# A graph network and attention kernel on one core: later steps for the aggregates and projections of two slots, and a gather moved ahead of a scatter

## What is computed

```python
h = jnp.maximum(_layernorm(x, axis=-1), 0.0)
x = x + _L0_gnn_ref(adj, h, L0_gnn_W, L0_gnn_b)      # gather of up to 25 rows, maximum, linear, relu
h = jnp.maximum(_layernorm(x, axis=-1), 0.0)
x = x + _L1_gnn_ref(h, adj, L1_gnn_Wqkv, ...)        # attention over adj | adj.T | eye, then the feed-forward part

# inside _L0_gnn_ref
scores = jnp.where(mask, pri, neg_inf)
vals, idx = jax.lax.top_k(scores, S)                 # S = 25: the lowest neighbour indices
feats = jax.vmap(lambda x, i: x[i])(X, idx)
agg = feats.max(axis=2)
out = jax.nn.relu(jnp.einsum('bnf,fo->bno', h, W) + b)

# inside _L1_gnn_ref
scores = jnp.where(allowed[:, None], scores, -jnp.inf)
attn = jax.nn.softmax(scores, axis=-1)
```

## Time and profile before

| | |
|---|---|
| timed executions, us | 1256.07, 1257.35, 1259.07; median 1257.35 |
| span of the profiled execution, us | 1257.3 (no other time is given for it; its span is within 0.05 of the median) |
| busy, share of the span | TensorE 84%, VectorE 64%, ScalarE 64%, GpSimd 59% |
| chain that ended last | TensorE 63%, ScalarE 11%, VectorE 9%, GpSimd 7%, issue 6%, DMA 3% |
| mean granted TensorE clock | 0.933 |

### The profile page before, as it was taken

How to read it: one execution, slowest core, us unless ns; L and a number is a source line. 1 busy time by engine, 2 the same in 40 slices (tenths; PEclk the granted TensorE clock), 3 DMA queues, 4 the chain that set the end, 5 groups by cost and what they waited for, 6 DMA issues and landing times.

```text
span 1257.3 us, 29309 instructions
## 1 busy us (share of the span) xinstructions
PE 1051.1 (84%) x10998; PEld 407.3 (32%) x10998; DVE 809.0 (64%) x3062; ACT 805.9 (64%) x1031; POOL 737.5 (59%) x741
## 2 busy tenths in 40 slices
PE   0136687688993989999999999999999999999874
PEld 0122331243331433343434333434343334333222
DVE  7866887758778476977797869776364534122323
ACT  1221257677852767788878887888768756875541
POOL 4776677567777777777777777777777520000000
PEclk9556789899997899999999999999999999999996
DMA  6523336416322534353435343532242210000000
GB/s 188 167 69 105 93 103 158 147 53 137 119 83 80 140 85 135 104 121 85 131 112 115 87 129 107 120 86 62 78 69 71 55 52 18 18 3 10 10 9 8
DMA packets 95157, 110.77 MB, mean 88 GB/s; under 512 B 17081, under 2 KB 75969, under 8 KB 94977
## 3 DMA queue, kind: packets, MB, share of 16 engines
q1 hardware_dynamic: 68352, 62.67, 16.4%
q0 software_dynamic: 22816, 44.61, 15.6%
q10 hardware_dynamic: 3808, 1.19, 0.4%
HBM read 91.10 MB, written 12.85 MB: 83 GB/s over the span
## 4 chain that ended last, share of the span: by engine, by line
PE 63%; ACT 11%; DVE 9%; POOL 7%; issue 6%; DMA 3%; DVEq 0%; POOLq 0%; ACTq 0%; SPq 0%
PE sc L1673 20%; PE cb L1693 13%; ACT probs L1469 10%; PE sc L1677 7%; PE m L1749 5%; PE m L1757 4%; POOL nb_low L716 3%; POOL nb_low L694 3%; PE m L1579 2%; PE m L1602 2%; PE sc L1715 1%; DMA nb_low<-h_rows,lsorted 1%; PE m L1731 1%; PE m L1607 1%; PE m L1779 1%
## 5 line engine op out<-in xcount | busy, mean ns | idle before, releaser
L1469 ACT ACTIVATE probs<-sc 128x1024 f32<-128x1024 f32 x512 | 496.5, 1022 | 247.6 <-PE sc L1677 245.6
L694 POOL DMA_INDIRECT nb_low<-h_rows,lsorted x474 | 470.1, 992 | 172.3 <-issue 126.1
L1693 PE MATMUL cb<-probs,va 128*17 128x512 f32 x2048 | 272.3, 604 | 4.8 <-issue 4.1
L1673 PE MATMUL sc<-q_near,k_g 32*128 32x512 f32 x1024 | 147.8, 644 | 21.7 <-ACT probs L1469 18.5
L1673 PE MATMUL sc<-q_far,k_g 32*128 32x512 f32 x1024 | 149.6, 654 | 16.3 <-ACT probs L1469 15.9
L1016 DVE TENSOR_REDUCE agg<-nb_low 128x128 f32<-128x1024 f32 (+10 forms) x58 | 96.4, 1662 | 54.3 <-DMA nb_low<-h_rows,lsorted 31.5
L1677 PE MATMUL sc<-barred,negident 32*32 32x512 bf16 x4096 | 112.9, 388 | 0.3 <-issue 0.2
L830 DVE MAX8 cand<-keys 128x8 f16<-128x128 f16 x512 | 105.4, 279 | 2.2
L716 POOL DMA_INDIRECT nb_low<-h_rows,first_lists x80 | 80.1, 1001 | 42.5 <-issue 23.2
L1677 PEld LDWEIGHTS sc<-barred,negident 32*32 32x32 bf16 x4096 | 35.4, 88 | 198.6 <-issue 198.6
L1461 ACT ACTIVATE barred<-m 128x512 bf16<-128x512 f32 x128 | 73.4, 610 | 40.6 <-PE m L1607 40.6
(11 more groups left out here) (182 smaller groups left out, 1457.6 us busy)
## 6 DMA issues: line engine op xcount, KB each, us to landing
adj_t<-in_adj_dram SPq DMA_DIRECT2D x64, 512.0 KB
nb_low<-h_rows,lsorted POOLq DMA_INDIRECT x474
xh<-in_x_dram SPq DMA_DIRECT2D x8, 512.0 KB
h_rows<-xh SPq DMA_DIRECT2D x8, 512.0 KB
hl<-h_rows SPq DMA_DIRECT2D x8, 512.0 KB
x<-in_x_dram SPq DMA_DIRECT2D x16, 256.0 KB
out_dram<-h2T SPq DMA_DIRECT2D x16, 256.0 KB
ag<-pooled_rows SPq DMA_DIRECT2D x7, 512.0 KB
```

The lines of the kernel that those rows point to most:

```text
L694: pool.indirect_dma_start(out=dst, out_offset=None, in_=h_rows[0:(f + 1) * (N + 1), :], in_offset=bass.IndirectOffsetOnAxis(ap=lsorted[:, ...
L1469: nc.scalar.activation(probs[:, i % 2, 2 * pair:2 * pair + 2, :], sc[:, 2 * pair:2 * pair + 2, :], ACT.Exp, scale=SCALE).then_inc(s_probs, 1)
L1673: nc.tensor.matmul(sc[:, a, :], k[part, :], q[part, :], start=True, stop=False)
L1693: last = nc.tensor.matmul(cb[a * SPAN:a * SPAN + VW, :], va[:, u % 2, a, kt, :], probs[:, i % 2, a, :], start=(kt == 0), stop=(kt == T - 1))
```

## The change

Six things are moved; no instruction is added or taken away except register instructions.

1. Slot 0, graph 1: the transposes of `ag` go from step 22 to 24, the linear layer from 23, 24 to 25, 26, the transposes behind it from 27 to 28, the projections from two a step in 28 and 29 to two a step in 29 and 30, the value rows from 30 to 31.
2. Slot 0, graph 2: the two TensorE steps of its ranks (the transpose of `full` and the rank counts) go from 19 and 21 to 21 and 23.
3. Slot 0, graph 3: ScalarE applies the first norm in steps 27 and 28, not 22 and 23 (`H_AT_0`), and on VectorE `first_norm(3)` stands behind `linear(1)`, not ahead of it; `list_tile(3, 2)` goes behind `flag(1)`, and the adjacency loads are set around `store_h_rows(3)` and `turn_values(1, 0)`.
4. Slot 1, graph 2: the transposes of `ag` go from step 20 to 23, the linear layer from 21, 22 to 24, 25, the transposes behind it from 25 to 27, the projections from one a step in 26 to 29 to two a step in 28 and 29.
5. Slot 1 on VectorE: `add_input(0, 1)` ahead of `pool_tile(2, 6)`, `list_tile(4, 2)` behind `pool_tile(2, 7)`, and graph 3's `pool_tile(3, 0)` and `(3, 1)` behind `flag(2)`.
6. GpSimd, graph 2 only: tile 7 is gathered ahead of `scatter_lists(3)`; the scatter is cut in two around `send(2, 7)`, and `load_lists(3)` follows it.

```diff
+H_AT_0 = {27: (0, 4), 28: (4, 8)}
+PROJ_AT_LATE = {29: [(0, 0), (1, 1)], 30: [(2, 2), (3, 0)]}
-RANK_AT = {0: (-2, 3, 7, 8), 1: (0, 0, 2, 4), 2: (0, 19, 21, None), 3: (1, 11, 12, None)}
+RANK_AT = {0: (-2, 3, 7, 8), 1: (0, 0, 2, 4), 2: (0, 21, 23, None), 3: (1, 11, 12, None)}
...
-    return {0: (5, 21, 25), 1: (22, 23, 27)}.get(f, (20, 21, 25))
+    return {0: (5, 21, 25), 1: (24, 25, 28), 2: (23, 24, 27)}.get(f, (20, 21, 25))
...
-    return PROJ_AT_1 if f == 1 else PROJ_AT
+    return {1: PROJ_AT_LATE, 2: PROJ_AT_1}.get(f, PROJ_AT)
+def values_at(f):
+    return 31 if f == 1 else 30
...
                         if f and t >= 2:
                             send(f, t - 2)
-                        if t == T - 2 and f >= AHEAD:
+                        if t == T - 2 and f > AHEAD:
                             if f + 1 < B:
                                 scatter_lists(f + 1)
                             beta2(f - 1)
+                    if f == AHEAD:
+                        send(f, T - 2)
+                        scatter_lists(f + 1, (0, TH))
+                        send(f, T - 1)
+                        scatter_lists(f + 1, (TH, T))
+                        beta2(f - 1)
...
                     join_first(1)
+                    linear(1)
                     first_norm(3)
-                    linear(1)
+                    context(0, 2)
                     list_tile(3, 0)
+                    bias_ahead(1)
                     list_tile(3, 1)
-                    merge_pair(0)
-                    context(0, 2)
-                    bias_ahead(1)
                     largest(1, 0)
                     largest(1, 1)
-                    list_tile(3, 2)
+                    merge_pair(0)
...
                     wide_maxima(1, 1)
+                    add_input(0, 1)
                     pool_tile(2, 6)
-                    add_input(0, 1)
-                    list_tile(4, 2)
                     finish(0, 1)
                     context(1, 1)
                     pool_tile(2, 7)
+                    list_tile(4, 2)
                     list_tile(4, 3)
```

More of the change, by code:

```diff
@@ L566, in first_slot @@
                     load_shift(0, 1)
+                    load_list_tile(3, 2)
                     store_h_rows(3)
-                    for t in range(2, 6):
-                        load_list_tile(3, t)
+                    load_list_tile(3, 3)
                     turn_values(1, 0)
+                    load_list_tile(3, 4)
+                    load_list_tile(3, 5)
                 prologue()
@@ L660, in load_lists, with scatter_lists @@
                     pool.dma_start(lsorted[:, k, :, :], rows_of(lists[k])).then_inc(s_lists_in, 16)
-                def scatter_lists(r):
+                def scatter_lists(r, tiles=(0, T)):
                     pool.wait_ge(s_ranks, 2 * (r + 1))
                     k = r % 2
-                    for t in range(T):
+                    for t in range(*tiles):
                         pool.wait_ge(s_scores, scatter_paced(r, t))
@@ L753, in _ @@
                             load_lists(f + 1)
-                        if f >= AHEAD:
+                        if f > AHEAD:
                             send(f, T - 2)
@@ L1261, in first_slot @@
                     flag(1)
+                    list_tile(3, 2)
                     list_tile(3, 3)
@@ L1372, in _ @@
                         low_levels(r)
-                    if live(r):
+                    if live(r) and s > 1:
                         pool_tile(r, 0)
@@ L1397, in _ @@
                         flag(f)
+                    if s == 1:
+                        pool_tile(r, 0)
+                        pool_tile(r, 1)
                     if live(r):
@@ L1543, in _ @@
                         if live(l) and l not in (0, 2):
-                            for t in range(*(H_AT if l > 4 else H_AT_1).get(n, (0, 0))):
+                            for t in range(*(H_AT if l > 4 else H_AT_0 if l == 3 else H_AT_1).get(n, (0, 0))):
                                 first_norm(l, t)
@@ L1895, in _ @@
                                 projection(f, j, bank)
-                            if n == 30:
+                            if n == values_at(f):
                                 value_rows(f)
```

2 lines of the change are left out of this document (1 added, 1 removed).

## The result

The changed kernel takes 1278.72 us (median of 4, 1277.26 to 1279.96), the kernel before 1256.71 (4 runs, 1255.47 to 1259.07): a ratio of 1.0169, interval [1.0151, 1.0186]. It is 22.0 us slower; 9.2 were forecast. The profiled execution after took 1277.26 us with a span of 1275.5, so 1.8 us lie outside the span; it was the shortest of the four, and its slot 0 opened at 159.59, 1.95 us earlier than in the execution before (161.54), a difference of the prologue and not of the change. The spans, 1275.5 and 1257.3, differ by 18.2. In every execution of this case for which both are known the time is 1.7 to 1.8 us above the span, so the span of 1257.3 belongs to the execution of 1259.07 us, the longest before, and its nearness to the median is chance.

What follows compares the result with a forecast made beforehand. GpSimd's back-to-back gathers were to gate TensorE early in slot 2 through `context(1, 3)`: 1257.3 + 7.8 (TensorE late) + 1.4 (lower clock) = 1266.5 us, range 1259 to 1272.

Steps and rivals of the forecast that it cites:

- S: Graph 3's first gather on GpSimd: forecast at 414.6 us, each microsecond past 406.8 being a microsecond of the end.
- VectorE at 7 us late: End of slot 0: VectorE 7 us late, as `first_norm` and two list tiles stand behind the last of it.
- A: Start of `add_input(0, 1)` on VectorE in slot 1: forecast at 386.3 us, 386.19 before.
- more than this: Rival: slot 0 longer than priced or another stop in slot 2, end at 1270 to 1274 us; 15 in 100.
- whose gathers GpSimd issues as before: Slot 1: VectorE's waits for gathers, 3.0 us and one like it, take off its 7 us, leaving about 2 to 3.
- `linear(1)` gets its input about 4 us earlier: Slot 0: earlier input to the linear layer, with h ready at 275 us, not 279.05.
- TensorE gains these 7.4 us: Slot 0: `full` needed two steps later, when it is ready at 243.2 us, so TensorE's 7.4 us wait goes.
- The ranks are VectorE's and come as before: Slot 0: GpSimd's scatter for graph 2 and its first gather, at 272.93 us, move by under 1 us.
- send 7 to S, 15.4: End of graph 2 on GpSimd: send, four scatters, `beta2`, load and its flight take 15.4 us, where it was 2.3.
- real and worth nothing: Slot 1: TensorE gains some 5 us, slot 2 opening near 457, but then waits for `context(1, 3)` in step 3.
- (3, 0) and (3, 1) behind `flag(2)` cost nothing: Slot 1, VectorE: moving graph 3's first two maxima is free, as their gathers end 10 us later anyway.
- The clock's 1.4: Slot 2: after its long wait TensorE runs at its lower clock, costing 1.8 us, of which 1.4 counted.

Runs made afterwards that it cites:

- 5b: The move of graph 3's first two maxima behind `flag(2)`; parts 4 and 5 alone on the kernel before took 1262.01 us with it, 1257.01 us without.
- the run meant for it: Kernel before with parts 1 and 3, `first_norm(3)` ahead of `linear(1)`, rank steps as before: ratio 1.0006, on the first slower chip 1.0055.

## Why the prediction was right and wrong

**Right: the direction and the chain in slot 2.** Slower; no wait for `ag`; TensorE stopped in step 3 of slot 2 behind `context(1, 3)`, behind the maxima of graph 3's tile 3, behind the list load. `context(1, 3)` ended 69.2 us after S (69.3). Send 7 started 12.6 us after `add_input` (12.9). ScalarE waited 9.8 us for the norm (about 10). The wait for `add_input` in step 17 stayed, at 6.2 us (9.2). From slot 2 on the shift was carried to the end, less 1.0 us. Part 6 alone cost 13.3 us, though with the stop in slot 1.

**The step that failed: "VectorE at 7 us late".** It measured 13.7 us at the first maximum of slot 1, and with it A was 392.9, not 386.3 (+6.6). The absorption was forecast rightly, and it was not what failed: 7 us were to shrink to 2.5, by 4.5, and 13.7 shrank to 9.3, by 4.4. VectorE's 7.0 us of waits for gathers went, and some 2.5 us of other waits came. But these waits could not give more than they held. Tile 6, no longer ahead, gave 2.6 us (2.4): 386.19 + 9.3 - 2.6 = 392.9. (Taken from slot 0's opening A is later still, by 2 us.) The bound of the rival "more than this" (390) was passed too. "Whose gathers GpSimd issues as before" did not hold either, since their waits for scores between 265 and 480 us grew from 9.3 to 13.8 us, but up to `add_input` no item of VectorE waited for one.

**Where the 13.7 us come from: slot 0.** "`linear(1)` gets its input about 4 us earlier" failed first. It began at 268.02, 2.0 us later than before (266.05). Its steps stand later, and "TensorE gains these 7.4 us" did not come: the wait for `full` gave way to 8.0 us for `context(0, 1)`, which the next mask count needs. With the rank steps back TensorE waits 8.7 us for `full` again, and `linear(1)` begins at 268.77; either way nothing is gained. From there on everything came 5 to 8 us later than forecast: h ready at 280.94 (275), ScalarE's norm at 286.10 (280.1), TensorE's step 29 at 289.61 (284), slot 1 at 307.89 (300 to 303). VectorE is 10.9 us late at `flag(1)` (306.22 against 295.35); the rest of the 13.7 is `list_tile(3, 2)`, which part 3 puts behind it. With parts 1 to 3 alone and the norm put back ahead of `linear(1)` VectorE is 3.5 us late at tile 0, and 3.3 to 4 us of time come back. Slot 0 alone measured +9.6 us, where I had given about 2.5 of it to A and nothing to TensorE. TensorE's own way was mispriced as well: it came to step 3 of slot 2 at 482.14, 6.0 us late, where 471 had been forecast. This costs nothing only because `context(1, 3)` came later still.

**Wrong within it: the ranks.** "The ranks are VectorE's and come as before" left out that they need the transpose of `full` and the counts from TensorE, whose steps had been moved: first gather +5.3, not under 1. By itself this cost nothing (1266.7 without it, 1266.8 with it), because VectorE, late by itself, waited for no gather in either. Whether it costs once the norm is put back stays open; the run meant for it is one of those on the slower chips.

**Wrong by size: send 7 to S, 15.4, measured 18.4 (+3.0).** The send took 1.96, not 1.0; the load stood 3.71 us, not 1.2. It waits for the last scatter to land. Slot 0, from which the 1.2 us were taken, could not price that: there the load follows `beta2` by 1.15 to 1.17 us in all fourteen profiled executions on the usual chips, so it shows no wait for the scatters. In the windows after, the DMA engines' share (the column before the last) is 0.05 during slot 0's scatter and 0.74 during slot 1's:

```profile
262.00:274.00 12.00, 12.00 (x141) 6.98 (x138) 1.70 (x4) 8.61 (x12) 9.00 (x9) 1.00 0.05 11
406.00:419.00 13.00, 9.17 (x116) 2.50 (x108) 11.81 (x47) 10.66 (x16) 8.05 (x7) 1.00 0.74 220
```

From the load to the first gather it was 5.0 us (5.2 taken from slot 0). That it fits so well is partly luck: with part 6 the stretch took 4.3 us in one execution and 7.1 in another, and in this one the profile names the store of graph 4's rows as what ended it. The estimate of 2.3 us for the load by the Trainium skill's page "DMA: Bandwidth & Descriptors" (Anatomy of one DMA) would have been further off; the trace has 3.6 us from its issue to landing.

**Missed: a wait of GpSimd for tile 5's maximum** ahead of the gather of tile 7 (3.5 us; "GpSimd, free at 375.7, gathers tile 7"). It cost nothing, since send 7 hangs on VectorE.

**Half right: slot 1's gain.** With parts 4 and 5 alone slot 2 opened 7.7 us early and step 3 took it back, as in the forecast's "real and worth nothing", but behind 5b and not behind part 6; without 5b only 0.75 us is gained. **"(3, 0) and (3, 1) behind `flag(2)` cost nothing"** held only while S was late: in slot 1 alone it is 5.0 us, 1262.0 against 1257.0.

The sum with the measured terms: 6.6 - 0.3 + 3.0 - 0.1 = 9.2 on top of 1266.5 is 1275.7, the span is 1275.5. The clock's 1.4 was 2.2 in steps 4 and 5, with 1.0 given back in the last slots. The median is 3.2 us above that span: 1.8 outside the span, which the forecast left out by adding its terms to a span and calling it the median's time, and 1.5 because this execution was the shortest of four, with the early prologue.

## What to carry to other kernels

A removed wait is worth nothing until the item behind the waiting one is named, on both engines: the 7.4 us for `full` became 8.0 us for `context(0, 1)`, and with the 10.6 us for `ag` gone slot 2 opened only 0.75 us earlier. The waits that an engine shows absorb a delay up to their own length and no further: VectorE's 7.0 us took 4.4 of 13.7. So the delay has to be sized first, and traced back to its start. A run that takes the time expected does not show the cause expected; look which engine waits for which in it. And put loads that others wait for ahead of work that waits itself: with two sends behind the list load GpSimd stood 0.30 us ahead of graph 3's first gather, with nothing behind it 4.06.
